# Adding the output biases of three attentions on GpSimd instead of TensorE

## What is computed

```python
x = x + xattn(layernorm(x), ctx, ...)
x = x + ffn(layernorm(x), ...)
```

```python
l1: out @ Wu.T + bu
l2: concat @ Wo.T + bo
l3: out @ Wo + bo        # V = value @ Wv + bv
```

## Time and profile before

| | us |
|---|---|
| median of 3 runs | 1032.79 (1032.47 to 1032.89) |
| span of the profiled execution | 1031.8 |
| TensorE, weight loads, VectorE, ScalarE, GpSimd busy | 857.6, 625.7, 749.6, 572.7, 437.1 |
| l1's loop and tail | about 192 to 280 |
| l2's loop and tail | about 433 to 514 |
| l3's loop and tail | about 922 to 1000 |

### The profile page before, as it was taken

The page is one execution under the profiler, slowest core; times in us unless marked ns, Lnnn a source line. Parts: engine busy times, 40 slices in busy tenths (PEclk is TensorE's granted clock), DMA queues, the critical chain, the costliest instruction groups (busy, mean ns, idle before and its releaser), DMA issues. The chain is left out here.

```text
span 1031.8 us, 26604 instructions
## 1 busy us (share of the span) xinstructions
PE 857.6 (83%) x10453; PEld 625.7 (61%) x10453; DVE 749.6 (73%) x1825; ACT 572.7 (56%) x1316; POOL 437.1 (42%) x286
## 2 busy tenths in 40 slices
PE   4274798889739996889878999999999999878888
PEld 3152554778526775545556777777777776644567
DVE  4989787678765544688797758576776758589974
ACT  4172244567615553467687484756648484246774
POOL 5000220597226776198205343342516253509820
PEclk9587899899959999899979999999999999899999
DMA  5411000400051112200010000000000000000001
GB/s 161 123 50 82 1 1 1 171 2 2 17 223 46 52 52 63 59 1 2 3 50 2 27 3 27 3 27 3 27 15 14 28 2 3 2 2 1 2 2 41
DMA packets 27127, 35.95 MB, mean 35 GB/s; under 512 B 7835, under 2 KB 20444, under 8 KB 26238
## 3 DMA queue, kind: packets, MB, share of 16 engines
q1 hardware_dynamic: 21310, 27.84, 8.4%
q0 software_dynamic: 2496, 5.12, 1.8%
q10 hardware_dynamic: 3200, 1.31, 0.5%
HBM read 26.98 MB, written 7.27 MB: 33 GB/s over the span
## 5 line engine op out<-in xcount | busy, mean ns | idle before, releaser
L2129 DVE TENSOR_TENSOR soft_outs<-soft_expert_ps,soft_bias 128x512 f32<-128x512 f32 x128 | 87.3, 688 | 89.5 <-PE soft_expert_ps L1847 89.5
L1847 PE MATMUL soft_expert_ps<-soft_W,soft_slots 128*32 128x128 f32 x4096 | 138.4, 278 | 9.7 <-issue 4.5
L1847 PEld LDWEIGHTS soft_expert_ps<-soft_W,soft_slots 128*32 128x32 f32 x4096 | 106.0, 110 | 40.7 <-issue 37.3
L1939 ACT ACTIVATE soft_slots<-soft_slot_ps 128x512 f32<-128x512 f32 x128 | 69.5, 594 | 85.2 <-PE soft_slot_ps L1833 83.5
L953 POOL TENSOR_TENSOR l_prob<-l_prob,l_inv 128x1024 f32<-128x1024 f32 x48 | 91.3, 1901 | 40.4 <-DVE l_inv L1107 39.0
L2024 POOL TENSOR_TENSOR l_ring<-l_ring,soft_inv 128x1024 f32<-128x1024 f32 x15 | 35.1, 2373 | 106.2 <-DVE soft_inv L2122 57.7
L1092 DVE TENSOR_REDUCE l_under<-l_score 128x16 f32<-128x1024 f32 x48 | 58.8, 1224 | 26.7 <-PE l_score L1173 14.4
L1794 PE MATMUL soft_slot_ps<-phi,xnT 128*128 128x256 f32 x256 | 69.3, 408 | 7.4 <-ACT soft_spread L1927 4.7
L1861 PE MATMUL soft_mix_ps<-soft_outs,soft_combT 128*64 128x128 f32 x1024 | 70.1, 279 | 1.5 <-DVE soft_acc L2145 1.5
L982 PE MATMUL l_turned<-ident,l_prob 128*128 128x128 f32 x384 | 52.4, 279 | 21.9 <-POOL l_prob L953 21.9
L1056 ACT ACTIVATE l_probT<-l_turned 128x512 f32<-128x512 f32 x96 | 52.1, 594 | 33.2 <-PE l_turned L982 33.2
(11 more groups left out here) (450 smaller groups left out, 2174.4 us busy)
## 6 DMA issues: line engine op xcount, KB each, us to landing
moe_w<-in_moe_W SPq DMA_DIRECT2D x2, 2048.0 KB, 10.1
soft_W<-in_soft_W SPq DMA_DIRECT2D x16, 256.0 KB, 2.8
kept<-early SPq DMA_DIRECT2D x1, 2048.0 KB, 6.3
l_keys<-in_moe_b SPq DMA_DIRECT2D x1, 2048.0 KB, 8.2
l_asked<-kept SPq DMA_DIRECT2D x1, 2048.0 KB, 13.0
ctxT<-in_ctxT SPq DMA_DIRECT2D x1, 1024.0 KB, 5.1
moe_rows<-xn_tok SPq DMA_DIRECT2D x4, 256.0 KB, 3.7
expert_rings<-moe_back SPq DMA_DIRECT2D x4, 256.0 KB, 6.1
```

The lines of the kernel that those rows point to most:

```text
L1847: last = nc.tensor.matmul(expert_ps[c][32 * j:32 * j + 32, h, tt, :], slots[u % 3][:, h, tt, 128 * c + 32 * j:128 * c + 32 * j + 32], W[i ...
L1939: last = nc.scalar.activation(slots[u % 3][:, h], slot_ps[h][:], ACT.Copy)
L2129: nc.vector.tensor_tensor(outs[u % 3][:, c].rearrange("p h t d -> p (h t) d"), expert_ps[c][:].rearrange("p h t d -> p (h t) d"), bias[i % ...
```

## The change

The bias products and the bf16 split go. The biases are now loaded as f32, repeated over all 128 partitions, and stay in SBUF. At the beginning of each attention loop, in turns 0 and 1, GpSimd adds the bias row to the rows of x, four tiles (128x512) in one instruction: two instructions in turn 0 and two in turn 1, behind `spread_keys` and ahead of `hide` and `share`. VectorE's `add` of a tile waits for the addition of its four tiles by the semaphore `biased`.

```diff
@@ warp
-            low, mid = slice(64, 65), slice(32, 33)
-            pool.wait_ge(core.loaded["biases"], 16)
-            pool.wait_ge(bias_taken, 1)
-            pool.wait_ge(path_done, 2)
-            nc.gpsimd.tensor_copy(core.bias16[:], core.biases[:]).then_inc(split_step, 1)
...
-            nc.gpsimd.tensor_copy(core.bias16[low], core.biases[low])
...
-            nc.tensor.matmul(last_bias, core.l3["bv"][:], core.l3["Wo_plain"][:], start=True, stop=False)
-            nc.tensor.matmul(last_bias, core.ident[0:65, 0:65], core.biases[:, 2, :], start=False, stop=True).then_inc(bias_made, 1)
+            nc.tensor.matmul(last_bias, core.l3["bv"][:].broadcast_to([128, 128]), core.l3["Wo_plain"][:], start=True, stop=False)
+            nc.tensor.matmul(last_bias, core.ident[:], core.biases[:, 2, :], start=False, stop=True).then_inc(bias_made, 1)
@@ attend
+            def add_bias(g):
+                rows = core.x[:, 4 * g:4 * g + 4, :]
+                nc.gpsimd.tensor_tensor(rows, rows, core.biases[:, bias, :].unsqueeze(1).broadcast_to([128, 4, D]), ALU.add).then_inc(biased, 1)
...
             for i in R:
                 if there(i + 3) and i + 3 >= prepared:
                     spread_keys(i + 3)
+                if i < 2:
+                    add_bias(2 * i)
+                    add_bias(2 * i + 1)
                 if beside:
                     beside(pool, i)
...
             def add(t):
                 dve.wait_ge(out_done, t + 1)
+                dve.wait_ge(biased, t // 4 + 1)
@@ l1_attention, output (head_attention alike)
-                nc.tensor.matmul(out[64 * j:64 * j + 64, 0:128], mixedT[:, j, 64 * a:64 * a + 64], wu[:],
-                                 start=(a == 0), stop=False)
-        return nc.tensor.matmul(out[:, 0:128], core.ones16[:], core.bias16[:, 0, :], start=False, stop=True)
+                last = nc.tensor.matmul(out[64 * j:64 * j + 64, 0:128], mixedT[:, j, 64 * a:64 * a + 64], wu[:],
+                                        start=(a == 0), stop=(a == 1))
+        return last
@@ prepare, layout
-    core.bias16 = sb("bias16", [65, 3, D], BF16)
+    core.biases = sb("biases", [128, 3, D])
...
-            w["bv"], w["bq"], w["bk"] = sb("l3_bv", [128, 65]), sb("l3_bq", [128, 1]), sb("l3_bk", [128, 1])
+            w["bv"], w["bq"], w["bk"] = sb("l3_bv", [128, 1]), sb("l3_bq", [128, 1]), sb("l3_bk", [128, 1])
...
-    out["biases"] = np.zeros((65, 3, D), np.float32)
-    out["biases"][::32] = np.stack([v["L1_xattn_bu"], v["L2_xattn_bo"], v["L3_xattn_bo"]])
+    out["biases"] = np.broadcast_to(np.stack([v["L1_xattn_bu"], v["L2_xattn_bo"], v["L3_xattn_bo"]]), (128, 3, D))
```

More of the change, by code:

```diff
@@ L307, in warp @@
         total_ps = st.ps("total", [128, 2 + D])
-        total, last_bias = total_ps[:, 0:2], total_ps[0:65, 2:2 + D]
+        total, last_bias = total_ps[:, 0:2], total_ps[:, 2:2 + D]
         sums_done, total_done, mean_done, per_mean_done = (st.sem("sums_done"), st.sem("total_done"), st.sem("mean_done"),
@@ L316, in warp @@
         keys_turned, values_done = st.sem("keys_turned"), st.sem("values_done")
-        bias_made, bias_taken, split_step = st.sem("bias_made"), st.sem("bias_taken"), st.sem("split_step")
+        bias_made, bias_taken = st.sem("bias_made"), st.sem("bias_taken")
         early_made, early_taken, kept_out = st.sem("early_made"), st.sem("early_taken"), st.sem("kept_out")
@@ L902, in _, with attend @@
                 nc.vector.tensor_copy(core.l1_asked[:, g, :, 0], by_head(norm.banks[g]))
-def attend(nc, core, name, score, value, output, mix_scale, spread, keys, prepared, next_norm, sets=1, loads=(), read=None,
+def attend(nc, core, name, score, value, output, bias, mix_scale, spread, keys, prepared, next_norm, sets=1, loads=(), read=None,
            on_act=None, on_dve=None, beside=None):
@@ L932, in attend @@
         mix_done, mixedT_done = st.sem("mix_done"), st.sem("mixedT_done")
-        out_done, added = st.sem("out_done"), st.sem("added")
+        out_done, added, biased = st.sem("out_done"), st.sem("added"), st.sem("biased")
         both = [bank[:].rearrange("p n s -> p (n s)") for bank in scores]
@@ L1205, in l1_attention @@
     attend(nc, core, "l1", score, lambda t, m: values[:, 2 * t + m // 4, m % 4].rearrange("p i k -> p (i k)"),
-           output, 0.5, lambda out, t: spread_sets(nc, core, out, t), ring, 2, "ln3", 2, loads, route_group, on_dve=take_gates, beside=hide)
+           output, 0, 0.5, lambda out, t: spread_sets(nc, core, out, t), ring, 2, "ln3", 2, loads, route_group, on_dve=take_gates, beside=hide)
 def choose_two(nc, st, dve, act_half, done, logits, first, weights, E):
@@ L1682, in output @@
             for b in range(2):
[L1683 to L1687, removed]
+                last = nc.tensor.matmul(out[64 * b:64 * b + 64, 0:128], mixedT[:, i, 64 * b:64 * b + 64], w["Wo"][:, b, i, :],
+                                        start=(i == 0), stop=(i == 1))
+        return last
+    attend(nc, core, name, score, lambda t, m: values[:, t, m], output, 1 if masked else 2, 1.0,
            lambda out, t: spread_heads(nc, core, queries.kT, out, t), queries.ring, 1 if masked else 4, next_norm, **read)
@@ L2475, in layout @@
     out["l2_Wo"], out["l3_Wo"] = v["L2_xattn_Wo"].T, v["L3_xattn_Wo"]
-    out["l3_bv"] = np.zeros((128, 65), np.float32)
-    out["l3_bv"][:, ::32] = np.asarray(v["L3_xattn_bv"])[:, None]
-    out["biases"] = np.zeros((65, 3, D), np.float32)
-    out["biases"][::32] = np.stack([v["L1_xattn_bu"], v["L2_xattn_bo"], v["L3_xattn_bo"]])
+    out["l3_bv"] = v["L3_xattn_bv"][:, None]
+    out["biases"] = np.broadcast_to(np.stack([v["L1_xattn_bu"], v["L2_xattn_bo"], v["L3_xattn_bo"]]), (128, 3, D))
     for key in ("l2", "l3"):
@@ L2569, in build @@
               nc.sbuf_tensor("conv_bias", [65, 512], F32) as core.conv_bias, nc.semaphore("loaded_bias") as bias_in,
-              nc.sbuf_tensor("biases", [65, 3, D], F32) as core.biases, nc.semaphore("loaded_biases") as biases_in):
+              nc.semaphore("loaded_biases") as biases_in):
             core.ctx_tok = ctx_tok
```

## The result

The changed kernel takes 1044.79 us (median of 4 runs, 1043.60 to 1048.07) against 1032.84 for the kernel before beside it (1032.47 to 1035.56): ratio 1.0114, 95% interval 1.0099 to 1.0128, slower by 12.0 us. Two further groups of runs gave 1044.66 against 1033.78 and 1043.81 against 1034.21, ratios 1.0101 (1.0087 to 1.0116) and 1.0094 (1.0080 to 1.0107). I had forecast slower, 1040.5 us, at most 1043.0. The direction and the places were right; the size was too small by 1.8 to 4.2 us: 12.0, 10.9 and 9.6 measured against 7.76. The 9.6 of the last group would lie inside my range, the other two above it.

The account below looks back on a forecast made before the run. The loops were taken as bound by a chain across engines, with additions delaying its start; l1 +2.00, l2 +6.08 and l3 -0.32 made +7.76 us on the median 1032.79, so 1040.5 us, range 1036.5 to 1043.0.

Parts of the forecast that it names:

- What bounds the loops: Attention loops: a chain across engines, not TensorE's load, sets the period; removing bias products leaves 8.59 and 8.36 us unchanged.
- The tails: Ends of the attentions: output products no longer wait for bias products, -0.32 us each, a further -0.16 in l2.
- Price of an addition: One 128x512 addition on GpSimd takes 1.19 us, so four at a loop's head take 4.76 us.
- 4.76 forecast: l2's head: no idle time covers the four additions, so the first scaling comes 4.76 us later.
- l3's head at 0: l3's head: GpSimd's waiting covers the additions, cost 0 with 0.3 us of cover left, up to +0.2.
- What was costed at nothing: Missing bias split, larger bias load, 128-row last-bias product and VectorE's second wait: 0, at most 0.6 us in l3.
- l1, head: 4.76 - 2.44: l1's head: four additions less GpSimd's 2.44 us wait before the first scaling, +2.32 us.
- I price the clock at 0: l1's head: GpSimd limits the first tiles, so TensorE's clock costs 0, up to 1.0 us.
- l2, clock: +1.8: l2's head: first transposes and scores run at the 1.2 GHz level, +0.89 us each, bounds 0 and 2.2.

Follow-up runs that it names:

- experiment 1: Changed kernel without its twelve additions, output biases left out: ratio 0.9983, again 0.9986; kernel before without its 48 bias products, biases left out: 0.9991.
- experiment 8: Changed kernel with l1's additions as one 128x512 in the head and twelve by tile, l2's sixteen by tile, l3's kept: 1033.06 us against 1034.21, ratio 0.9993.
- 2nd: Second profile of the changed kernel, run again unaltered in a later group: 1044.66 us against 1033.78 for the kernel before, ratio 1.0101.
- 3rd: Third profile of the changed kernel, run again unaltered in the last group: 1043.81 us against 1034.21 for the kernel before, ratio 1.0094.
- experiments 2: Changed kernel with additions in one attention only, the other two biases left out: l1 only 1.0023, l2 only 1.0082 of the kernel before.
- experiment 3: Changed kernel with filler products on TensorE in l2's third turn: 88 gave ratio 1.0083, 118 gave 1041.29 us against 1033.78, ratio 1.0071.
- l2 alone: Changed kernel with the additions only in the second attention, the other two biases left out: ratio 1.0082 to the kernel before.
- the late write: Kernel before plus one late wait and 128x1 write by GpSimd at the end of the stage ahead of l2: 1044.59 us, ratio 1.0096.
- experiment 6: Changed kernel with l1's and l2's additions cut to one per tile, four turns after the tile's own, l3's kept in the head: 1037.86 us, ratio 1.0035.
- experiment 7: Changed kernel with filler products on TensorE in the third turn, 76 in l1 and 118 in l2: 1039.66 us against 1034.21, ratio 1.0056.
- experiment 4: Changed kernel with l2's and l1's first three additions in the stages before: 1043.20 us, 1.0093; kernel before with one late GpSimd write: 1044.59 us, 1.0096.

## Why the prediction was right, and where it failed

- **What bounds the loops: right.** The periods stand, the product's time became a wait, and without products and additions the kernel gains 0.9991 and 0.9986, the tails' part. The tails gave what was forecast: l3's 0.33 us, l2's 0.49 from the 15th scaling to the next stage, and l1's 0.32 from the 16th scaling to the last addition to x (7.80 or 7.81 us in eleven profiles without the products, 8.12 and 8.13 in two with them) where the clock held there.
- **Price of an addition: near.** 1.25 us, not 1.19; the step on GpSimd from an addition to the next instruction is 1.23. l2's first scaling came 4.80 us later after the block's start (4.76 forecast), l1's 2.53 (2.32). The Trainium skill's figure (GPSIMD Engine Reference, section 3) led to an estimate of 1.1 to 1.3; by it, the trace agrees.
- **l3's head at 0: right**, 0.20 us of cover left.
- **What was costed at nothing** (the split, the loads, the wider product, VectorE's second wait): right, by experiments 1 and 8.
- **"l1, head: 4.76 - 2.44": failed in part.** I took the idle time of one execution for a property of the kernel. 1.3 us of it were there because the opening scores had met a low clock; in executions without that, 7.9 us are enough for the first scaling, and the additions' 11.74 lose 3.8, not 2.5. On the mean of the eight profiles of experiment 1 it is 2.8.
- **"I price the clock at 0" in l1: the step that failed.** I argued that GpSimd limits the first tiles. It does, but TensorE's idle time of 3.7 to 5.1 us in the head had low stretches behind it, which cost 0.24 to 1.16 us up to the third scaling, and in two of the three profiles another 0.7 to 1.3 up to the 16th. From the block's start to the 16th scaling, six profiles with l1's additions at its head and no filler there (after, 2nd, 3rd, experiments 2 and 3) have 77.42 us on the mean, and six without (before, the three of experiment 1, l2 alone, the late write) 73.80: +3.6 where I had 2.32.
- **"l2, clock: +1.8": too small.** 2.2 in the head in all three profiles (I had it as the upper bound), and in the 3rd, as in the run with l2 alone, a second stretch behind it that took the third to the 16th scaling from 52.80 to 54.11. Block to 16th scaling: 76.28 us on the mean of four with the additions, 68.71 of five without: +7.6 where I had 6.4.

Together these two make 2.5 us of the miss, which was 3.1 on the mean of the three groups. Another 0.4 lies in l1's tail, which I had not priced for the clock: its last addition to x came 8.58, 7.80 and 8.32 us behind the 16th scaling in the three profiles of the changed kernel, and 7.81 with the head filled, where the clock held. What is left is too small to be placed: the step from l2's 16th scaling to l3's block, with no part of the change in it, alone went from 416.5 to 420.3 us between two executions of the changed kernel, the granted clock from 516 to 916 us being 0.99 and 0.98 on the mean. My range took in the clock's costs as one event for each head, and its upper end, at 1043.0, was the sum of one each; what the runs show is that a longer idle time also has a second low stretch behind it in some of the executions.

The Trainium skill (TensorE: Matmul & The Clock Gate, Part 1) says that the same kernel meets a different number of slow products from run to run, puts the slow start under 1% of a typical kernel's span, and advises against fitting to a count. Here the variation is seen, and the clock's 4.2 us were 0.4% of the kernel but over a third of the change's effect.

## What to carry over

Here work put ahead of the first link of the chain was paid in full but for the idle time that stood there, whatever GpSimd's mean load; the same work went for nothing in the loop's own free time (0.85 us for two tiles in l2), cut to fit and done two turns before its reader (experiment 8). Queued one turn before, it made the reader wait at the loop's end (experiment 6). Count with it what the idle engine loses afterwards: TensorE's clock fell behind the lengthened wait in l1's and l2's head in every profile that had one, and filler products gave it back where they filled the wait (118 of them in experiment 3, and experiment 7), not where they left 2.01 us of it (the 88 of experiment 3). An idle time read off one execution is a cover only as far as other executions have it, so look what clock ran ahead of it.

## What the runs showed of the hardware that was not expected

- GpSimd's closing instruction of the stage with the gathers and scatters lasts 6.4 to 6.5 us behind its last work, even behind a write of 0.10 us (experiment 4). In the attention stages it shows 2.0 us, but starts there with the last scaling of 1.90 us, so that it ends 0.1 us behind GpSimd's last work. Why it is longer in this stage was not tried.
- An addition of 128x128 on GpSimd takes 0.46 us and of 128x512 1.25, steps of 0.41 and 1.23: about 2.1 ns for each further element. The scaling of 128x1024, which repeats each value over a row segment, takes 1.90, so the same engine is faster for it than for two additions of 128x512.
- 0.34 us of idle time behind 118 filler products left the clock at 1.00; 2.01 us behind 88 did not (experiment 3), and 1.66 us went without a fall in the kernel before. The length of the idle time alone doesn't decide it: behind the same 2.22 us l1's opening scores took 3.81 us in one execution and 5.44 in another (experiment 1).
